# Work moved from VectorE to GpSimd and ScalarE in a fused two-layer attention and feed-forward kernel

## The reference

```python
x = x + xattn0(_layernorm(x), ctx, Wq, bq, Wk, bk, Wv, bv, Wo, bo)
x = x + ffn0(_layernorm(x), gate_w, gate_b, val_w, val_b, out_w, out_b)
x = x + xattn1(_layernorm(x), ctx, mask)
x = x + ffn1(_layernorm(x), w_gate_up, w_proj)
```

## Time and profile before

| | |
|---|---|
| median of 3 runs | 829.83 us (825.33 to 831.72) |
| span of the profiled execution | 828.8 us |
| own time of that execution | not given apart from its span |
| busy: PE, DVE | 759.6 us (92%), 739.1 us (89%) |
| busy: ACT, POOL | 699.6 us (84%), 636.2 us (77%) |
| transfers | 82.59 MB, mean 100 GB/s |

### The profile page before, as it was taken

How to read it: one execution, slowest core, us unless ns; L and a number is a source line. 1 busy time by engine, 2 the same in 40 slices (tenths; PEclk the granted TensorE clock), 3 DMA queues, 4 the chain that set the end, 5 groups by cost and what they waited for, 6 DMA issues and landing times. The chain is left out here.

```text
span 828.8 us, 22129 instructions
## 1 busy us (share of the span) xinstructions
PE 759.6 (92%) x6898; PEld 397.6 (48%) x6898; DVE 739.1 (89%) x1636; ACT 699.6 (84%) x1447; POOL 636.2 (77%) x1139
## 2 busy tenths in 40 slices
PE   2588999999999999999999999999999999998876
PEld 1233344444455554555555555555554545444444
DVE  3898798999999999999999999999999999987765
ACT  3788987988899898999898989999998888887644
POOL 3765656778898888988888888888888887777632
PEclk9555898999999999999999999999999999999999
DMA  8410222344434444544445444444444445434230
GB/s 287 140 54 19 71 67 64 76 105 94 112 87 108 109 110 110 108 116 112 104 111 116 112 101 110 109 105 106 117 101 120 99 91 115 95 87 91 57 72 20
DMA packets 197952, 82.59 MB, mean 100 GB/s; under 512 B 139710, under 2 KB 196670, under 8 KB 197836
## 3 DMA queue, kind: packets, MB, share of 16 engines
q1 hardware_dynamic: 193260, 74.63, 38.5%
q10 hardware_dynamic: 4576, 6.55, 2.4%
HBM read 28.15 MB, written 4.69 MB: 40 GB/s over the span
## 5 line engine op out<-in xcount | busy, mean ns | idle before, releaser
L1141 DVE TENSOR_REDUCE mx<-psS 128x2 f32<-128x512 f32 x512 | 334.1, 680 | 21.8 <-PE psS L630 20.2
L813 ACT ACTIVATE prob<-psT 128x512 f32<-128x512 f32 x512 | 292.5, 604 | 27.0 <-PE psT L638 21.6
L630 PE MATMUL psS<-KQ 31*128 31x256 f16 x1024 | 137.6, 285 | 7.0 <-DVE mx L1141 3.6
L652 PE MATMUL psW<-prob,vst 128*32 128x256 f32 x2048 | 143.0, 400 | 0.1
L741 PE MATMUL psW<-guT,xT 128*128 128x512 bf16 x512 | 132.6, 387 | 6.2 <-DMA xT<-stage 5.3
L638 PE MATMUL psT<-KQ 32*128 32x256 f16 x1024 | 130.4, 280 | 4.0 <-ACT prob L813 3.1
L652 PEld LDWEIGHTS psW<-prob,vst 128*32 128x32 f32 x2048 | 55.0, 112 | 61.4 <-issue 34.6
L741 PEld LDWEIGHTS psW<-guT,xT 128*128 128x128 f16 x512 | 43.1, 99 | 71.5 <-issue 36.5
L1025 POOL TENSOR_TENSOR hqB<-wide,rnd 128x512 bf16<-128x512 f32 x60 | 63.1, 1056 | 13.6 <-ACT wide L863 13.4
L1039 POOL TENSOR_TENSOR stage<-stage 128x512 f16<-128x512 f32 x60 | 69.7, 1162 | 2.5 <-ACT stage L924 1.8
L630 PEld LDWEIGHTS psS<-KQ 31*128 31x128 f16 x1024 | 40.4, 93 | 64.2 <-DVE mx L1141 38.0
(11 more groups left out here) (191 smaller groups left out, 1779.1 us busy)
## 6 DMA issues: line engine op xcount, KB each, us to landing
KQ<-hl SPq DMA_DIRECT2D x192, 64.0 KB, 1.9
xP<-in_x SPq DMA_DIRECT2D x32, 128.0 KB, 2.3
cP<-in_ctx SPq DMA_DIRECT2D x32, 128.0 KB, 2.1
xA<-in_x SPq DMA_DIRECT2D x32, 128.0 KB, 2.7
cB<-in_ctx SPq DMA_DIRECT2D x32, 128.0 KB, 2.3
oV<-uA SPq DMA_DIRECT2D x32, 128.0 KB, 2.1
out<-x SPq DMA_DIRECT2D x32, 128.0 KB, 2.0
oR<-rden_d SPq DMA_DIRECT2D x120, 32.0 KB
```

The lines of the kernel that those rows point to most:

```text
L630: m = nc.tensor.matmul(psS[:, n % 2, T * k:T * k + T], KQ[p % DEEP][r, 1, g, 128 * k:128 * k + 128], KQ[p % DEEP][r, 0, g, :], start=True, ...
L652: m = nc.tensor.matmul(bank[32 * j:32 * j + 32, :], vst[p % DEEP][:, k, 4 * n + j, :], prob[:, (4 * n + j) % 8, k, :], start=(k == 0), sto ...
L813: m = nc.scalar.activation(flat(prob[:, n % 8, :, :]), psT[:, n % 2, :], ACT.Exp, scale=float(HC) ** -0.5)
L1141: m = nc.vector.tensor_reduce(mx[:, p % 2, :, 4 * (n % 4) + n // 4], psS[:, n % 2, :].rearrange("p (c s) -> p c s", c=NK), AX.X, ALU.max)
```

## The change

- **Cosine product.** r1 goes from VectorE to GpSimd. ScalarE gets a second bias copy, pn, which reads proj0 and frees its bank.
- **First norm.** xnP goes from ScalarE to GpSimd. All four norms become one tensor_scalar on GpSimd, (x + nm) * rs, with nm the negated mean, made in the step rs before.
- **Scale products.** sxB loses two products and sx two. A new step gs on GpSimd makes three scales from sxB's result, a new step os the output scale. tB waits for gs, sx for gs, x2 for os.
- **Rounding.** hq subtracts its constant as one tensor_scalar.
- **Clips and fills.** cl, ct and the two later fills of vst go from VectorE to GpSimd.
- **Weight scale.** The factor of hC is made a power of two and multiplied into the up weights, in the copies tc2 and tc3, which wait for gv; hC becomes a plain product.
- **Context.** A transposed context is an input of its own, loaded per pair into a double buffer by a new transfer cT (128x256). xcT makes two transposes instead of four and its copy halves; sc waits for cT, ro for cB.
- **Maxima.** They lie in one 128x32 tile, so mxp is one transpose; its copy is 32x128 instead of 16x256.
- **Squares.** sq is one pass over 1024 after hC1. ms has one tensor_scalar and one power; rs one power with an exponent per row.
- **Orders.** ORDER, HEAD and TAIL are new for all engines. LOOP is the same. gm stands ahead of the first score in HEAD, where it stood behind S9:0. gs, os, r1 and xnP are in GpSimd's list, pn in ScalarE's, cT in SP's.

```diff
-READER: "proj0": "r1"
+READER: "proj0": "pn"
 ...
+                elif name == "cT":
+                    after_apart(sp, "sc", p - 2)
+                    sp.dma_start(cT[:, p % 2, :, :], ctx_t[p]).then_inc(S[("cT_even", "cT_odd")[p % 2]], 16)
 ...
-                    for k in range(NK):
-                        m = nc.tensor.transpose(bank[0:NH, 128 * k:128 * k + 128], mx[:, p % 2, k, :], ident)
+                    m = nc.tensor.transpose(bank[0:NH * NK, 0:128], flat(mx[:, p % 2, :, :]), ident)
 ...
-                    after_dma(pe, "cB", p)
-                    for c in range(2 * NK):
-                        m = nc.tensor.transpose(bank[:, 128 * c:128 * c + 128],
-                                                (xnD, cB)[c // NK][:, 128 * (c % NK):128 * (c % NK) + 128], ident)
+                    for c in range(NK):
+                        m = nc.tensor.transpose(bank[:, 128 * c:128 * c + 128], xnD[:, 128 * c:128 * c + 128], ident)
 ...
+                elif kind in ("pn", "pc"):
+                    by, dst, i = {"pn": ("r1", pn, 0), "pc": ("r2", pc, 1)}[kind]
+                    after(act, "proj", p, i)
+                    after(act, by, p - 1)
+                    for f in range(2):
+                        m = nc.scalar.activation(dst[:, T * f:T * f + T], psW[:, BANK[f"proj{i}"], T * f:T * f + T],
+                                                 ACT.Identity, bias=qkb[:, 2 * f + i:2 * f + i + 1])
 ...
                     if n == 0:
-                        after(act, "sxB", p)
+                        after(act, "gs", p)
 ...
-                    inner(1, nc.gpsimd.tensor_tensor(centre[:], src[:], mv[:, 0:1].broadcast_to([P, T]),
-                                                     ALU.subtract))
-                    m = nc.gpsimd.tensor_tensor(dst[:], centre[:], rs[:, 1:2].broadcast_to([P, T]), ALU.mult)
+                    m = nc.gpsimd.tensor_scalar(dst[:], src[:], nm[:], rs[:, 1:2], ALU.add, ALU.mult)
 ...
+                elif kind == "gs":
+                    sc = sB[:, p % 2, :]
+                    after(pool, "sxB", p)
+                    after(pool, "tB", p - 2, 1)
+                    after(pool, "sx", p - 2)
 ...
+                    nc.gpsimd.tensor_scalar(sc[:, 4:5], sc[:, 1:2], gam_q[:, 0:1], 1.0, ALU.mult, ALU.mult)
+                    nc.gpsimd.tensor_scalar(sc[:, 7:8], sc[:, 1:2], sc[:, 1:2], gam_q[:, 2:3], ALU.mult, ALU.mult)
+                    m = nc.gpsimd.tensor_scalar(sc[:, 5:6], sc[:, 2:3], sc[:, 2:3], gam_q[:, 1:2], ALU.mult, ALU.mult)
+                elif kind == "os":
+                    after(pool, "sx", p)
+                    after(pool, "x2", p - 2)
+                    m = nc.gpsimd.tensor_scalar(sc[:, 9:10], sc[:, 6:7], sc[:, 7:8], 1.0, ALU.mult, ALU.mult)
 ...
-                    m = nc.gpsimd.tensor_tensor(hqB[:, h], hrB[:, h], rnd[:].broadcast_to([P, 512]), ALU.subtract)
+                    m = nc.gpsimd.tensor_scalar(hqB[:, h], hrB[:, h], -ROUND, 1.0, ALU.add, ALU.mult)
 ...
-                    inner(1, nc.gpsimd.tensor_tensor(sD[:, 3:4], sD[:, 2:3], mone[:], ALU.pow))
-                    m = nc.gpsimd.tensor_tensor(sD[:, 4:5], sD[:, 3:4], valid[:, p:p + 1], ALU.mult)
+                    m = nc.gpsimd.tensor_tensor(sD[:, 4:5], sD[:, 2:3], expo[:, p:p + 1], ALU.pow)
```

## The result

The changed kernel takes **849.53 us** (median of 4 runs, 844.81 to 853.1), the kernel before on the same chip 827.58 (4 runs, 823.84 to 831.72). The ratio is **1.0241, 95% interval 1.0169 to 1.0313**: slower by 2.4%. I had predicted 804 (788 to 830) with 0.72 on faster. The profiled execution spans 844.7 us against 828.8 before.

The account below looks back on a forecast made before the run. TensorE was taken to lead, fed late by chains through other engines and transfers and coupled to VectorE. Span 828.8, loop -24, head +1, tail -2 gave 803.8, plus 1.0 to run time 804.8; put at 804, range 788 to 830.

Parts of the forecast that it names:

- The busy terms: Busy time per pair after the change: TensorE 21.4 us, VectorE 19.6 to 19.9, ScalarE 20.0, GpSimd 19.0.
- The first maximum: Head: the first score maximum would come at 37.5 us instead of 32.04, 5.5 later.
- Rival 2: GpSimd's in-order loop queue becomes the bound: 856 us, or 841 with less wait; chance 0.12.
- The loop ... I give back a third: Loop: of 1.52 us coupling a pair, 0.5 returns; with TensorE's 0.31 the pair takes 21.6, saving 24 us.
- My own sign for being wrong: Loop: TensorE's idle per pair stays as before while VectorE's grows by all it saved.
- Rival 1: The coupling stays: TensorE's waits end with transfers whose landing no edit shortens; 820 us, give or take 5; chance 0.20.
- r1: Cosine product moved to GpSimd: per pair +1.27 us there, +0.84 on ScalarE for copies, -0.87 on VectorE.
- the added waits: New dependences on GpSimd's scale steps: tB0 behind gs has some 1.5 us of cover, so costed at nothing.
- the queues: SP's queue: one more transfer a pair and reordered loads, taken at nothing, bounded by 0.6 us a pair.
- the head: Start of the program: first maximum 5.5 us later, less 4.5 of VectorE relief; net +1 us, bounds -6 and +12.
- The head's upper end: Head costs +12 us if the clips on GpSimd hold up lo and the key transfers.
- The context's loaded transpose and the single transpose of the maxima: TensorE's loop: 0.21 and 0.10 us saved, together 0.31 a pair, 9 us over 29.5 pairs.

Follow-up runs that it names:

- e8: The change's contents in the old orders on all engines, with clips, fills and cosine product back on VectorE, no ScalarE copy: 815.7 us, 0.9867 of the kernel before.
- e6: The change's contents in the old orders, with the clips, ternary clips and two fills back on VectorE: 828.54 us, 1.003 of the kernel before.
- e7: The change's contents in the old orders, with the cosine product back on VectorE and no ScalarE copy; clips stay on GpSimd: 820.32 us, 0.993 of the kernel before.
- e3: All contents of the change, with the orders of the kernel before on every engine: 834.78 us, 1.0106 of the kernel before.
- e14: The change in its new orders, with the cosine product back on VectorE, read from the projection's bank: 857.54 us, 1.0349 of the kernel before.
- e10: As e8, but the cosine product on VectorE reads ScalarE's copy instead of the bank: 864.47 us, 1.0474 of the kernel before.
- e1: The change with T0 later in TensorE's loop, behind pv3, S2, S3 and sc: 863.31 us, 1.0462 of the kernel before.
- e5: The change with u1 ahead of the tanh of C on ScalarE and pv3 right behind pv2 on TensorE: 858.09 us, 1.0382 of the kernel before.
- e13: As e5, with SP's load cP also moved from the loop's front to behind ht: 899.96 us, 1.0832 of the kernel before.
- e9: The change with the old order put back on SP's queue alone: 888.52 us, 1.0778 of the kernel before.
- e11: As e8, with the context transposed by TensorE again and no load of the transposed tile: 815.77 us, 0.9897 of the kernel before.
- e2: The change with the maxima as before, a 16x256 tile, two transposes and larger transfer pieces: 850.45 us, 1.03 of the kernel before.
- e16: The kernel before with one edit, the rounding on GpSimd as one two-operation instruction: 821.3 us, 0.9917 of the kernel before.
- e12: As e8, with the first norm put back on ScalarE: 814.29 us, 0.9886 of the kernel before.
- e15: The kernel before with two GpSimd edits, each norm one subtract-and-multiply instruction and the rounding one two-operation instruction: 817.21 us, 0.9876 of the kernel before.

## Why the prediction was wrong

**The ledger.** In per cent of about 827 us: contents without the two moves -1.3, cosine product +1.7, clips +0.7, orders +1.35. Sum +2.4, the measured 2.4; in us about -11, +14, +6 and +11. The terms are differences along one path of runs (before, e8, e6 or e7, e3, the change), so they add up by construction, and each holds in the orders in which it was taken: the product's +1.7 in the old ones. In the new lists putting it back gained nothing (e14).

**What held.** The busy terms. GpSimd was forecast at 19.0 us a pair and is at 19.2: its rounding at 0.65 came out as 0.652, the norms at 0.45 were too low at 0.558, the small scales at 0.267 as 0.26 to 0.35. ScalarE was put at 20.0 and is; VectorE at 19.6 to 19.9, and is 20.1; TensorE at 21.4, and is 20.9. The first maximum was late, though by 2.4 us and not 5.5. Rival 2, GpSimd as the bound, has 841 to 856 us and so holds the measured time, but by luck: its mechanism is not there, 401.67 of 480 us busy is less than the 414.71 before.

**First failed step: "The loop ... I give back a third".** I read the earlier trace rows as coupling that a lighter VectorE would loosen. The forecast was 21.6 us a pair, 24 us less in all; the measured pair takes 22.9, and the changed kernel is 8 maxima, 11 us, behind in the 480 us of the window. My own sign for being wrong came true: VectorE's idle grew and TensorE's did not fall, it rose from 0.70 to 2.0. Rival 1 gave the mechanism, transfers and gates that no lighter engine shortens, but only as no gain; I left out that the coupling could tighten.

**Second: "r1" costed as busy time alone.** In the prediction the cosine product is +1.27 on GpSimd, +0.84 on ScalarE and -0.87 on VectorE, which reads as a cheap trade. I did write that the bank of proj0 is now freed by pn, and then asked only after keys that come late. A later user of that bank is Bd on TensorE. In the old orders that is where the cost shows: 8.8 us more idle time ahead of Bd in e6 than in e8, beside 8 us lost in the same window and 13 us between the two medians. The work of the product went to the engine with the most idle time, and the gate went to ScalarE, into a list of 40 steps. That this gate is the whole price is argued from the waits, not shown by a run. In the changed kernel itself TensorE waits for pn there only once, 0.3 us: its new lists have this gate covered, and what they lose, they lose elsewhere (below). e10 shows that whoever waits for the copy matters more than who multiplies: with VectorE behind it the kernel takes 36 us more than with GpSimd behind it.

The Trainium skill (GPSIMD Engine Reference, Engine selection) advises against two-input elementwise work on this engine, about twice as slow as on VectorE. The rows agree in direction only: 1.271 us against two halves of 0.476 in the earlier trace rows is 1.3 times, and I was wrong to read the like of it as agreement with twice. On the same shape, from SBUF, VectorE took 0.674 to 1.762 us in e10, median 0.981: GpSimd's 1.27 is 1.3 times the median and 1.9 times the shortest. Whether GpSimd's slowness costs time here, no run separates. One-input work at roughly line-rate, the other half of that advice, depends here on the form: 0.558 us in one and 1.243 in another, at the same shape.

**Third: the added waits and the queues "at nothing".** For tB0 behind gs that was right: no wait of tB0 for GpSimd stands among the waits of 200 to 680 us, so the 1.5 us of cover held. For the new orders it was wrong. I checked the reserves that the added dependences need, not those that the permutation removed: T0's distance from mxp (7.1 us before, 5.5 with the wait) and u1 behind two exponentials, with ov behind it. For the keys I had counted 4 us less reserve and priced it at nothing; the scores' loads now wait 12.3 us for them instead of 4.2. Together the orders cost 11 us. Which exchange in them does it is open: removing the wait for the maxima alone (e1), both waits (e5) or both holders of SP's queue (e13) made it worse, SP's old order does not fit the new lists (e9), and no run put back the order of another single engine.

**Fourth: the head.** I priced the clips' departure as 4.5 us of relief for VectorE and let their arrival on GpSimd reach only the upper bound. They cost 1.9 us each there (1.05 and 0.93 on VectorE), ahead of the key and weight steps, and 0.7% of the time. The head's upper end of +12 was the nearer one: 9 maxima, 13 us, are missing by 200 us, part of it from the orders.

**Terms without effect.** The context's loaded transpose and the single transpose of the maxima, 0.31 us a pair on TensorE, which I multiplied by 29.5 into 9 us, show no gain (e11 against e8, e2 against the change), though the intervals leave room for most of it. And of the gain of 1.3% that there is, a line that I entered only in GpSimd's busy sum, the rounding, gives 0.8% by itself (e16).

## What to carry to other kernels

When work moves between engines, price the gate that moves with it: who frees the bank now, from which place of which in-order list, and what stands on the tensor engine behind that bank. A price found so holds in the lists in which it was found (e7 and e8 against e14). In a loop where all engines are 86 to 97% busy by hand-written lists, a wait in the profile is where lateness shows and need not be where it arises; three times here (e1, e5, e13), removing a large new wait made the kernel slower. Take such a change apart before keeping it: one edited line of it alone gives 0.8% (e16), and e8 and e12, the contents with old orders and VectorE's work left in place, are 1.3% and 1.1% faster than before while the whole change is 2.4% slower.

## What the runs showed of the hardware

- **One shape, two prices on GpSimd.** A 128x256 f32 tensor_scalar with two per-partition scalars took 0.558 us as add and multiply and 1.23 to 1.24 as subtract and multiply (rows of the change and e15). The first scalar also lies differently, a column of its own against a column of a two-column tile, and no run separates the two.
- **Two operations with constants against a second input.** 128x512 f32 to bf16 took 0.62 to 0.65 us as tensor_scalar and 1.056 with a broadcast second input.
- **VectorE's product of two SBUF inputs varies.** 128x512 f32 took 0.674 to 1.762 us, median 0.981, over the 32 of e10; what stretches the long ones was not looked into.
- **VectorE's smallest instructions stretched.** Five of the six of bs took 0.33 to 1.74 us from 35.05 to 40.30, the sixth 0.17, while GpSimd ran 2048 columns of bf16 products and a clip from 34.31 to 40.35; in the kernel before, at 71.45 us, the same six took 0.17 to 0.23 each. That GpSimd's work is the cause is only suggested by the two rows falling together; no run separates it.
